# Sixty-four experts spread over 28 steps instead of 32, and eight output tiles normalised in a new order

## The chip, the cores and the metric

The kernel runs on one core of one Trainium2 chip. The metric is the device time of one execution in microseconds (us). A core has five engines with a program each: TensorE (PE, matmuls), VectorE (DVE), ScalarE (ACT), GpSimd (POOL) and SyncE (SP, which here only issues DMAs). They meet at semaphores: an instruction waits until a counter has reached a value, and raises another when it is done. Sixteen DMA engines move data for all of them.

## What is computed

A layer of a network on `x`, 4 sequences of 1024 tokens with 512 channels, so 4096 rows in all. First comes an attention-like part (a linear recurrence over time), with a norm and a residual; its result is called `x1`, and its layernorm `h`. The change touches only the second part, the feed-forward:

```
idx, wts = router(h)                       # 64 experts, 6 chosen for each token, weights wts
shared = relu2(h @ shared_up.T) @ shared_down.T          # 512 -> 1024 -> 512, every token
routed = for each expert e: its tokens (at most 128) through relu2(xd @ w1[e].T) @ w2[e].T,
         times wts, added into the row of each token     # 512 -> 256 -> 512
out = x1 + layernorm(shared + routed)
```

`relu2` is the square of relu. The sum over a token's experts and the shared part is formed in an array `ysh` in HBM and in SBUF, as told below.

## The kernel before

**Tiles and steps.** The 4096 rows are 8 row tiles of 512, each 4 sub-tiles of 128. The shared part runs over the tiles `k = 0..7`, and in each over 8 slices `j = 0..7` of the hidden 1024. One pass over `j` is a step here: TensorE does `up(k, j)` (12 matmuls, since each product is split into three of high and low parts), ScalarE takes relu and square (L980, L985), VectorE the square and the low part (`split`, L1607 and L1610), and two steps later TensorE does `down(k, j-2)` (12 matmuls) into `y_bank`. The last two `down` of a tile follow in its last step.

**Experts.** From tile 3 on (`ROUTED`), the experts are woven into the steps. `experts_until(step)` shares the 64 evenly over steps `FIRST_STEP` to `LAST_STEP`, 2 to 33, counted from tile 3 slice 0; so every step has exactly two, and the last are in tile 7, slice 1. One expert is: POOL gathers 128 token rows of `h` by an indirect DMA (L1170); TensorE transposes them (L661), multiplies by w1 (L672, 16 instructions in the profile) and by w2 (L683, 4); ScalarE copies, takes relu, and scales by the gate (L1008, L1014, L1022); VectorE squares and writes the lists of indices (L1633, L1624, L1626, L1617); then POOL adds the 128 result rows into `ysh` with a second indirect DMA (L1196).

**What orders the adds.** Two experts can have the same token, so each add waits on `added` until the one before has landed: on POOL the program is gather, add, gather, add, and the adds are strictly one behind the other. There are four result buffers (`EB`) and four sets of weights (`WB`). VectorE's L1624 for expert e waits for the add of expert e-4, ScalarE's L1022 likewise. The gather of expert e+5 stands just ahead of the add of expert e in POOL's program. SP loads the w1 half (512 KB) of expert e+5 when expert e+1 is through its first matmuls, and the w2 half of e+4 when e is done.

**The end.** When all 64 adds have landed (`added` = 16*64), the sum of a tile k can be made whole. The shared results of tiles 0 to 2 are already in `ysh`; those of tiles 3 to 6 lie in SBUF (`v_sb`, `hb`, `sr`, `xin`), that of tile 7 in PSUM. Before the change, tiles 0 to 2 are just loaded; 3 and 4 come by DMAs of POOL that add while they land (`add_sums`, L1207); 7, 5 and 6 are summed by TensorE with an identity matrix (`o_sum`, L750 and L751). Then per tile, in the order of `O_ORDER`: VectorE takes mean and variance (`o_moments`, L1705 to L1711), POOL the inverse deviation (L1216, L1218), ScalarE normalises (`o_norm`, L1083), POOL and VectorE add `x1`, two sub-tiles each (L1226, L1719), and SP stores. VectorE's first three `o_moments` stand in steps j = 5, 6, 7 of tile 7, each behind that step's `split`, and `o_add(n)` stands behind `o_moments(n+1)`. The last `down(7, 7)` waits for the `split` of step 7.

Of the kernel before, what the change touches and what calls it, by code (L numbers as in the profile page):

```python
# [35 lines left out]
FIRST_STEP, LAST_STEP = 2, SJ * (NT - 1 - ROUTED) + 1  # L36
TURN_STEP = {1: 0, 2: 3, 3: 6, 4: 9, 5: 12, 6: 14, 7: 18}

O_ORDER = [0, 1, 2, 3, 4, 7, 5, 6]
O_ADDED, O_SUMMED = (3, 4), (7, 5, 6)  # L40
# [6 lines left out]
def sandwich(nc, t):  # L47

    ctx = ExitStack()
    with ctx:  # L50
# [170 lines left out]
        def by_row_tile(w):  # L221
            return w.rearrange("p (s c) -> p s c", s=ST)

        o_y = [hT, xres[:, :, :], xnd[:, :, :], v_sb[:, :, :], hb[:, :, :]] + [by_row_tile(weights[:, n, :]) for n in (5, 6, 4)]
        o_from = o_y[:5] + [banks[0], y_bank, y_bank]
        o_x = [by_row_tile(wkv[:, n * ST * C:(n + 1) * ST * C]) for n in range(WB - 1)] + [by_row_tile(state_flat[:, 0:ST * C])] + \
              [by_row_tile(weights[:, n, :]) for n in (7, 0, 1)] + [rw[:, :, :]]
# [7 lines left out]
        out_by_tile = t["out"].rearrange("(t s p) c -> t p s c", s=ST, p=P)  # L235

# [65 lines left out]
        def _(sp):  # L302
# [121 lines left out]
            def load_x1(k):  # L424
                sp.dma_start(o_x[k], x1_by_tile[k]).then_inc(S[f"x1_loaded{k}"], 16)

            def load_sums(k):
                sp.dma_start(o_y[k], ysh_by_tile[k]).then_inc(S[f"ysh_loaded{k}"], 16)
# [36 lines left out]
            load_x1(7)  # L465
            store_out(1)
            sp.wait_ge(S["down_done"], SJ * NT)
            load_x1(5)
            store_out(2)
            load_x1(6)  # L470
            for n in range(3, NT):
                store_out(n)
            sp.wait_ge(S["out_stored"], 16 * NT)
# [3 lines left out]
        def _(pe):  # L477
# [262 lines left out]
            def o_sum(n, k):  # L740

                pe.wait_ge(S[f"ysh_loaded{k}"], 16)
                if k == 5:
                    pe.wait_ge(S["relu_ready"], SJ * NT)
                    pe.wait_ge(S["e_gated"], E)
                if k == 6:
                    pe.wait_ge(S["o_normed"], ST * (O_ORDER.index(7) + 1))
# [8 lines left out]
            for n, k in enumerate(O_SUMMED):  # L756
                o_sum(n, k)
# [3 lines left out]
        def _(act):  # L761
# [326 lines left out]
            for n in range(2, NT):  # L1088
                o_norm(n)
# [672 lines left out]
```

## Time and profile before

| what | us |
|---|---|
| median of the runs | 1297.98 |
| the runs shown | 1286.64, 1297.98, 1530.0 |
| the profiled execution | 1293.94 |
| its span, first to last instruction | 1292.3 |
| TensorE busy | 1174.3 (91%) |
| VectorE busy | 770.2 (60%) |
| adds of experts (L1196), first issue to last | 774.75 to 1221.79 |
| stores and norms at the end, after the last add landed | about 65 |

Times in the trace are from the start of the span. The span is what the rows add up to; the profiled execution's own time is 1.64 us more.

### The profile page before, as it was taken

The numbers are of one execution on the slowest core, as the hardware profiler recorded it, in microseconds if no ns is written. First come the engines' busy times: TensorE is split into PE (matmuls) and PEld (weight loads), VectorE is DVE, ScalarE is ACT, GpSimd is POOL, SyncE is SP. The second block draws the span as 40 slices with busy tenths as digits, with TensorE's granted clock in tenths as the row PEclk, the third lists the DMA queues.
The fourth block names the chain that finished last, engine by engine and source line by source line (L and its number), as shares of the span: only waits on it lengthen the run. The fifth ranks groups of instructions, "written<-read, shape, count | busy, mean of one in ns | idle before, by whom it ended". The sixth has DMA issues, their size and how long they took to land.

```text
span 1292.3 us, 15333 instructions
## 1 busy us (share of the span) xinstructions
PE 1174.3 (91%) x4952; PEld 765.3 (59%) x4952; DVE 770.2 (60%) x1965; ACT 595.8 (46%) x993; POOL 283.4 (22%) x268
## 2 busy tenths in 40 slices
PE   5997999999889995869999899999998999999974
PEld 2443444443334442458888777777776777777751
DVE  4598988988798998759898941222221222222274
ACT  2455657574757557753333133343342334334243
POOL 2010202020202001200000023333342433433255
PEclk9998999999999998879999999999999999999987
DMA  8401022322222222596424149879988898997698
GB/s 299 179 1 33 11 75 66 97 46 98 32 93 37 83 48 98 138 289 213 159 86 155 39 154 242 243 218 268 240 205 256 228 244 235 246 244 174 161 309 341
DMA packets 79517, 206.16 MB, mean 160 GB/s; under 512 B 10192, under 2 KB 10320, under 8 KB 76624
## 3 DMA queue, kind: packets, MB, share of 16 engines
q1 hardware_dynamic: 59408, 156.98, 35.8%
q0 software_dynamic: 20032, 48.24, 19.4%
q8 instruction: 37, 0.61, 0.2%
q14 instruction: 40, 0.33, 0.1%
HBM read 145.93 MB, written 59.28 MB: 159 GB/s over the span
## 4 chain that ended last, share of the span: by engine, by line
PE 37%; DMA 11%; DVE 6%; issue 2%; ACT 1%; POOL 1%; SPq 1%; POOLq 0%; DVEq 0%; ACTq 0%
PE bank L672 7%; PE bank L683 7%; DMA ysh<-k_sb,mixf 5%; PE bank L647 3%; PE bank L649 3%; PE bank L648 3%; DMA xres<-h,mixf 3%; PE bank L629 3%; PE bank L631 3%; PE bank L630 3%; PE bank L661 2%; DMA xnd<-ysh 2%; PE bank L491 1%; DMA xin<-h 1%; DVE stats L1705 1%
## 5 line engine op out<-in xcount | busy, mean ns | idle before, releaser
L534 PE MATMUL bank<-mix_ring,weights 128*128 128x512 f32 x768 | 344.2, 606 | 13.7 <-ACT xres L835 6.7
L534 PEld LDWEIGHTS bank<-mix_ring,weights 128*128 128x128 f32 x768 | 147.5, 194 | 199.4 <-issue 192.9
L1196 POOL DMA_INDIRECT ysh<-k_sb,mixf x64 | 102.0, 1594 | 225.3 <-DVE mixf L1617 135.2
L1607 DVE TENSOR_TENSOR k_sb<-k_sb 128x512 f32<-128x512 f32 x64 | 44.1, 688 | 152.9 <-ACT k_sb L980 142.7
L1633 DVE TENSOR_TENSOR run_max<-run_max 128x256 f32<-128x256 f32 x64 | 27.3, 426 | 175.6 <-ACT run_max L1014 175.5
L541 PE MATMUL bank<-weights,rw 128*128 128x512 f32 x256 | 117.5, 614 | 12.1 <-ACT sr L794 9.0
L647 PE MATMUL bank<-ffn_w,s_split 128*128 128x512 f32 x256 | 115.1, 450 | 5.4 <-DVE s_split L1610 5.4
L629 PE MATMUL bank<-h_high,ffn_w 128*128 128x512 f32 x256 | 114.1, 446 | 4.3 <-ACT k_sb L980 2.7
L980 ACT ACTIVATE k_sb<-bank 128x512 f32<-128x512 f32 x64 | 38.2, 597 | 170.8 <-PE bank L631 170.8
L649 PE MATMUL bank<-ffn_w,s_split 128*128 128x512 f32 x256 | 101.8, 398 | 0.0
L648 PE MATMUL bank<-ffn_w,s_split 128*128 128x512 f32 x256 | 101.7, 397 | 0.0
L631 PE MATMUL bank<-h_high,ffn_w 128*128 128x512 f32 x256 | 100.8, 394 | 0.0
L630 PE MATMUL bank<-h_low,ffn_w 128*128 128x512 f32 x256 | 100.4, 392 | 0.0
L1170 POOL DMA_INDIRECT xres<-h,mixf x48 | 48.7, 1014 | 228.3 <-DVE mixf L1617 213.8
L672 PE MATMUL bank<-xnT,wkv 128*128 128x128 f32 x768 | 96.2, 280 | 0.1
L541 PEld LDWEIGHTS bank<-weights,rw 128*128 128x128 f32 x256 | 50.1, 198 | 77.1 <-issue 65.4
L1107 POOL TENSOR_SCALAR rstd<-mv 128x4 f32<-128x4 f32 x16 | 9.9, 620 | 379.8 <-DVE mv L1259 371.7
L672 PEld LDWEIGHTS bank<-xnT,wkv 128*128 128x128 f32 x768 | 92.3, 197 | 0.3 <-issue 0.3
L683 PE MATMUL bank<-wkv,run_max 128*128 128x512 f32 x192 | 90.3, 593 | 0.0
L1022 ACT ACTIVATE k_sb<-bank,mixf 128x512 f32<-128x512 f32 x64 | 44.1, 689 | 86.3 <-PE bank L683 78.3
L1288 DVE SCALAR_TENSOR_TENSOR mix_ring<-xnd,vecs,xnT 128x512 f32<-128x512 f32 x96 | 70.1, 745 | 3.9 <-PE bank L534 1.9
L1008 ACT ACTIVATE xnT<-bank 128x512 f32<-128x512 f32 x64 | 37.7, 588 | 66.9 <-PE bank L661 66.8
(217 smaller groups left out, 2025.5 us busy)
## 6 DMA issues: line engine op xcount, KB each, us to landing
wkv<-in_w SPq DMA_DIRECT2D x96, 512.0 KB
state<-in_w SPq DMA_DIRECT2D x32, 512.0 KB
xin<-in_x SPq DMA_DIRECT2D x8, 1024.0 KB, 5.3
xin<-h SPq DMA_DIRECT2D x8, 1024.0 KB, 6.4
xres<-in_x POOLq DMA_DIRECT2D x7, 1024.0 KB, 9.4
h<-hb SPq DMA_DIRECT2D x7, 1024.0 KB, 4.3
x<-xres SPq DMA_DIRECT2D x7, 1024.0 KB, 7.0
ht<-xnT SPq DMA_DIRECT2D x7, 1024.0 KB, 8.5
```

Of the source, the lines that this page charges most:

```text
L534: mm = pe.matmul(bank[:, d, :], W(j)[:, ck, d * P:(d + 1) * P], mix_slot(4 * j + ck), start=(ck == 0), stop=(ck == CK - 1))
L541: mm = pe.matmul(bank[:, s, :], rw[:, ck, s * P:(s + 1) * P], W(3)[:, ck, :], start=(ck == 0), stop=(ck == CK - 1))
L629: pe.matmul(up_bank, hi, hT_hi[:, ck, :], start=(ck == 0), stop=False)
L630: pe.matmul(up_bank, hi, hT_lo[:, ck, :], start=False, stop=False)
L631: mm = pe.matmul(up_bank, lo, hT_hi[:, ck, :], start=False, stop=(ck == CK - 1))
L647: pe.matmul(y_bank[:, s, :], hi, w_hi, start=(j == 0), stop=False)
L648: pe.matmul(y_bank[:, s, :], hi, w_lo, start=False, stop=False)
L649: mm = pe.matmul(y_bank[:, s, :], lo, w_hi, start=False, stop=(j == SJ - 1 and k < NT - 1))
L672: mm = pe.matmul(e_up_bank[:, i * CAP:(i + 1) * CAP], w1_sb[e % WB][:, ck, i * P:(i + 1) * P], xdT[q][:, ck, :], start=(ck == 0), stop=(ck ...
L683: mm = pe.matmul(route_bank, e_act[b][:, i, :], w2_sb[e % WB][:, i, :], start=(i == 0), stop=(i == IK - 1))
L1196: pool.indirect_dma_start(t["ysh"], bass.IndirectOffsetOnAxis(ap=scatter_token[:, q:q + 1], axis=0), e_out[q], None, compute_op=ALU.add).t ...
L1288: dve.scalar_tensor_tensor(out=mix_slot(n), in0=xnd[:, ck, :], scalar=vecs[:, MK + j, ck:ck + 1], in1=xnT[:, ck, 0:TT], op0=ALU.mult, op1= ...
```

## The change

`LAST_STEP` falls from 33 to 29, so the 64 experts lie in 28 steps, two in most and three in eight of them; the last three are in tile 6, slice 5. The end goes through the tiles in the order 0, 3, 4, 1, 5, 2, 6, 7. Tiles 3 and 4 are loaded plainly into the free buffers of tiles 1 and 2 and added to the shared result by VectorE (`O_JOINED`, a new counter `o_joined`); tiles 1 and 2 are loaded into those buffers once they are free again. Tiles 5 and 6 come by POOL's adding DMAs (`O_ADDED`), issued behind the first `o_scale`. Only tile 7 is summed by TensorE, straight onto its PSUM bank. `x1` passes through four slots. VectorE's first six `o_moments` stand in steps j = 2 to 7 of tile 7, and ScalarE's `o_norm` from j = 3.

```diff
-FIRST_STEP, LAST_STEP = 2, SJ * (NT - 1 - ROUTED) + 1
+FIRST_STEP, LAST_STEP = 2, SJ * (NT - 2 - ROUTED) + 5
-O_ORDER = [0, 1, 2, 3, 4, 7, 5, 6]
-O_ADDED, O_SUMMED = (3, 4), (7, 5, 6)
+O_ORDER = [0, 3, 4, 1, 5, 2, 6, 7]
+O_JOINED, O_ADDED = (3, 4), (5, 6)
...
+        o_y = [hT, xres[:, :, :], xnd[:, :, :]] + [m[:, :, :] for m in youts[ROUTED:]] + [by_row_tile(weights[:, 4, :])]
+        o_from = o_y[:NT - 1] + [y_bank]
+        x1_slots = [by_row_tile(wkv[:, n * ST * C:(n + 1) * ST * C]) for n in range(WB - 1)] + [by_row_tile(state_flat[:, 0:ST * C])]
+        sums_of = dict(enumerate(o_y))
+        sums_of.update({3: o_y[1], 4: o_y[2]})
...
             sp.wait_ge(S["added"], 16 * E)
-            for k in range(ROUTED):
-                load_sums(k)
-            sp.wait_ge(S["up_done"], SJ * NT)
-            load_sums(7)
-            load_x1(4)
-            load_sums(5)
-            store_out(0)
-            load_sums(6)
...
+            load_sums(0)
+            load_sums(3)
+            load_sums(4)
+            sp.wait_ge(S["o_joined"], ST)
+            load_sums(1)
+            sp.wait_ge(S["o_joined"], ST * 2)
+            load_sums(2)
+            for n in range(NT):
                 store_out(n)
+                if n + WB < NT:
+                    load_x1(n + WB)
+                if n == 2:
+                    sp.wait_ge(S["up_done"], SJ * NT)
+                    load_sums(7)
...
-            for n, k in enumerate(O_SUMMED):
-                o_sum(n, k)
+            pe.wait_ge(S[f"ysh_loaded{NT - 1}"], 16)
+            for s in range(ST):
+                mm = pe.matmul(y_bank[:, s, :], ident[:, :], sums_of[NT - 1][:, s, :], start=False, stop=True)
+            mm.then_inc(S["o_summed"], 1)
...
-                    if k == NT - 1 and j >= SJ - 2:
-                        o_norm(j - (SJ - 2))
+                    if k == NT - 1 and j >= 3:
+                        o_norm(j - 3)
...
             for n in range(NT):
                 o_scale(n)
+                if n == 0:
+                    for k in O_ADDED:
+                        add_sums(k)
...
-                    if k == NT - 1 and j >= SJ - 3:
-                        o_moments(j - (SJ - 3))
-                    if k == NT - 1 and j >= SJ - 2:
-                        o_add(j - (SJ - 2))
+                    if k == NT - 1 and j >= 2:
+                        o_moments(j - 2)
+                    if k == NT - 1 and j >= 3:
+                        o_add(j - 3)
...
+                if k in O_JOINED:
+                    dve.wait_ge(S["yout_ready"], ST * (k + 1))
+                    for s in range(ST):
+                        dve.tensor_tensor(o_y[k][:, s, :], o_y[k][:, s, :], sums_of[k][:, s, :], ALU.add).then_inc(S["o_joined"], 1)
+                    dve.wait_ge(S["o_joined"], ST * (O_JOINED.index(k) + 1))
```

The first place is ScalarE's program in a step of tile 5: one step before the change. `k_sb<-bank0` and `s_split` are the shared part; each row that waits on `added` is the gate of one expert, after which POOL can add its rows into `ysh`.

```order
L980 ACTIVATE k_sb_61<-bank0 128x512 [waits square_ready,up_done]
L985 ACTIVATE s_split_52<-k_sb_61 128x512 [waits down_done,relu_ready]
L1008 ACTIVATE xnT_59<-bank0 128x512 [waits e_up,xd_turned]
L1014 ACTIVATE run_max_65<-bank0 128x256 [waits e_square,e_up]
L1022 ACTIVATE k_sb_61<-bank0,mixf_60 128x512 [waits added,scatter_index,e_down]
L1008 ACTIVATE xnT_59<-bank0 128x512 [waits e_up,xd_turned]
L1014 ACTIVATE run_max_65<-bank0 128x256 [waits e_square,e_up]
L1022 ACTIVATE k_sb_61<-bank0,mixf_60 128x512 [waits added,scatter_index,e_down]
```

And one of the eight steps with three experts, after the change:

```order
L971 ACTIVATE k_sb_61<-bank0 128x512 [waits square_ready,up_done]
L976 ACTIVATE s_split_52<-k_sb_61 128x512 [waits down_done,relu_ready]
L999 ACTIVATE xnT_59<-bank0 128x512 [waits e_up,xd_turned]
L1005 ACTIVATE run_max_65<-bank0 128x256 [waits e_square,e_up]
L1013 ACTIVATE k_sb_61<-bank0,mixf_60 128x512 [waits added,scatter_index,e_down]
L999 ACTIVATE xnT_59<-bank0 128x512 [waits e_up,xd_turned]
L1005 ACTIVATE run_max_65<-bank0 128x256 [waits e_square,e_up]
L1013 ACTIVATE k_sb_61<-bank0,mixf_60 128x512 [waits added,scatter_index,e_down]
L999 ACTIVATE xnT_59<-bank0 128x512 [waits e_up,xd_turned]
L1005 ACTIVATE run_max_65<-bank0 128x256 [waits e_square,e_up]
L1013 ACTIVATE k_sb_61<-bank0,mixf_60 128x512 [waits added,scatter_index,e_down]
```

A third expert stands in the same step, and each of its three gates still waits for the adds of earlier experts.

The second place is VectorE's program at the end, where the second tile of `O_ORDER` is taken: before the change in step j = 6 of tile 7 (`xres` is tile 1, `xnT` tile 0).

```order
L1607 TENSOR_TENSOR k_sb_61<-k_sb_61 128x512 [waits relu_ready]
L1610 TENSOR_TENSOR s_split_52<-k_sb_61,s_split_52 128x512 [waits s_hi_ready,square_ready]
L1705 BN_STATS stats_71<-xres_57 128x6 [waits ln4_moments,ysh_loaded1]
L1705 BN_STATS stats_71<-xres_57 128x6 x3
L1708 BN_AGGR mv_72<-stats_71 128x2 [waits ln4_stats]
L1708 BN_AGGR mv_72<-stats_71 128x2 x3
L1710 TENSOR_SCALAR rstd_73<-mv_72 128x4 [waits ln4_moments]
L1711 TENSOR_SCALAR offset_76<-mv_72 128x4
L1719 TENSOR_TENSOR xnT_59<-xnT_59,wkv_67 128x512 [waits o_normed,x1_loaded0]
L1719 TENSOR_TENSOR xnT_59<-xnT_59,wkv_67 128x512 [waits o_normed]
```

After the change it stands in step j = 3, and is tile 3 (`v_sb`), whose routed part has landed in `xres`:

```order
L1599 TENSOR_TENSOR k_sb_61<-k_sb_61 128x512 [waits relu_ready]
L1602 TENSOR_TENSOR s_split_52<-k_sb_61,s_split_52 128x512 [waits s_hi_ready,square_ready]
L1694 TENSOR_TENSOR v_sb_62<-v_sb_62,xres_57 128x512 [waits yout_ready,ysh_loaded3]
L1694 TENSOR_TENSOR v_sb_62<-v_sb_62,xres_57 128x512 x3
L1702 BN_STATS stats_71<-v_sb_62 128x6 [waits ln4_moments,o_joined]
L1702 BN_STATS stats_71<-v_sb_62 128x6 x3
L1705 BN_AGGR mv_72<-stats_71 128x2 [waits ln4_stats]
L1705 BN_AGGR mv_72<-stats_71 128x2 x3
L1707 TENSOR_SCALAR rstd_73<-mv_72 128x4 [waits ln4_moments]
L1708 TENSOR_SCALAR offset_76<-mv_72 128x4
L1716 TENSOR_TENSOR xnT_59<-xnT_59,wkv_67 128x512 [waits o_normed,x1_loaded0]
L1716 TENSOR_TENSOR xnT_59<-xnT_59,wkv_67 128x512 [waits o_normed]
```

Four adds of 128x512 (L1694) have come between the `split` and the moments, and three more steps of the shared part now stand behind this place.

## Rows read from the trace of the kernel before

**Rows 1.** The page: TensorE's busy time; DMA busy tenths in 40 slices.

```profile
PE 1174.3 (91%) x4952; PEld 765.3 (59%) x4952; DVE 770.2 (60%) x1965; ACT 595.8 (46%) x993; POOL 283.4 (22%) x268
DMA  8401022322222222596424149879988898997698
```

**Rows 2.** Chain of waits, 1015:1035: start us, us, what. TensorE's pace.

```profile
1018.29 1.79 PE bank L672 x16
1024.98 1.79 PE bank L672 x16
```

**Rows 3.** Chain of waits, 1110:1250: three of the last five adds.

```profile
1192.65 8.02 DMA ysh<-k_sb,mixf
...
1201.53 7.70 DMA ysh<-k_sb,mixf
...
1221.79 4.82 DMA ysh<-k_sb,mixf
```

**Rows 4.** Timeline of POOL, adds of experts: start, us, line, [idle before <-releaser].

```profile
774.75 1.65 POOL L1196 DMA_INDIRECT ysh<-k_sb,mixf  x1 [0.30 <-issue]
...
859.38 1.59 POOL L1196 DMA_INDIRECT ysh<-k_sb,mixf  x1 [0.39 <-issue]
868.27 1.59 POOL L1196 DMA_INDIRECT ysh<-k_sb,mixf  x1 [5.33 <-DVE mixf L1617]
879.81 1.59 POOL L1196 DMA_INDIRECT ysh<-k_sb,mixf  x1 [8.66 <-DVE mixf L1617]
```

**Rows 5.** Line L1196 in the stretches 879:968 and 1120:1188: count, first and last start.

```profile
L1196 POOL DMA_INDIRECT ysh<-k_sb,mixf x14: 1587/1589/1605, 879.8 to 966.8; - x14
...
L1196 POOL DMA_INDIRECT ysh<-k_sb,mixf x11: 1587/1589/1590, 1120.5 to 1186.8; - x11
```

**Rows 6.** Timeline of ACT: gates of the first expert, the 61st, 62nd, and last.

```profile
772.10 0.69 ACT L1022 ACTIVATE k_sb<-bank,mixf 128x512 f32<-128x512 f32 x1 [1.34 <-PE bank L683]
...
1192.46 0.69 ACT L1022 ACTIVATE k_sb<-bank,mixf 128x512 f32<-128x512 f32 x1 [1.33 <-PE bank L683]
1196.40 0.69 ACT L1022 ACTIVATE k_sb<-bank,mixf 128x512 f32<-128x512 f32 x1 [1.34 <-PE bank L683]
...
1205.46 0.69 ACT L1022 ACTIVATE k_sb<-bank,mixf 128x512 f32<-128x512 f32 x1 [2.14 <-PE bank L683]
```

**Rows 7.** Timeline of ACT: relu in steps without experts.

```profile
1213.64 0.60 ACT L980 ACTIVATE k_sb<-bank 128x512 f32<-128x512 f32 x1 [4.18 <-PE bank L631]
...
1219.08 0.60 ACT L980 ACTIVATE k_sb<-bank 128x512 f32<-128x512 f32 x1 [4.18 <-PE bank L631]
```

**Rows 8.** Waits in 760:1227: who waited for whom, us in total, times, longest.

```profile
DVE mixf L1624 <- DMA ysh<-k_sb,mixf: 37.6, 32, 6.6
...
PE bank L661 <- DMA xres<-h,mixf: 10.3, 6, 4.4
```

**Rows 9.** Stretches: PE, PEld, DVE, ACT, POOL busy, PEclk, DMA share, GB/s.

```profile
1120.00:1186.00 66.00, 66.00 (x350) 51.20 (x349) 14.88 (x48) 22.26 (x41) 26.18 (x20) 1.00 0.89 235
...
1227.00:1252.00 25.00, 19.08 (x74) 14.94 (x73) 15.69 (x39) 8.20 (x12) 9.90 (x9) 0.86 1.01 272
```

**Rows 10.** Timeline of DVE from 1226: the end.

```profile
1232.26 2.47 DVE L1705 BATCH_NORM_STATS2 stats<-xnT 128x6 f32<-128x512 f32 x4 [5.69 <-DMA xnT<-ysh]
...
1235.34 0.68 DVE L1607 TENSOR_TENSOR k_sb<-k_sb 128x512 f32<-128x512 f32 x1
...
1244.31 1.79 DVE L1610 TENSOR_TENSOR s_split<-k_sb,s_split 128x512 fp32r<-128x512 f32 x1
...
1255.88 2.46 DVE L1705 BATCH_NORM_STATS2 stats<-hb 128x6 f32<-128x512 f32 x4
...
1260.19 2.47 DVE L1705 BATCH_NORM_STATS2 stats<-bank 128x6 f32<-128x512 f32 x4
...
1276.88 2.49 DVE L1705 BATCH_NORM_STATS2 stats<-bank 128x6 f32<-128x512 f32 x4 [8.03 <-PE bank L751]
```

**Rows 11.** Timeline of POOL: an add of x1 in the same stretch.

```profile
1244.29 2.94 POOL L1226 TENSOR_TENSOR xnT<-xnT,wkv 128x512 f32<-128x512 f32 x2
```

More of the change, by code:

```diff
@@ L222, in by_row_tile @@
             return w.rearrange("p (s c) -> p s c", s=ST)
[L224 to L227, printed above, removed]
+        o_y = [hT, xres[:, :, :], xnd[:, :, :]] + [m[:, :, :] for m in youts[ROUTED:]] + [by_row_tile(weights[:, 4, :])]
[3 more added lines that the diff above has]
+        sums_of.update({3: o_y[1], 4: o_y[2]})
         x_by_tile = t["x"].rearrange("(t s p) c -> t p s c", s=ST, p=P)
@@ L235, in sandwich, with o_x @@
         out_by_tile = t["out"].rearrange("(t s p) c -> t p s c", s=ST, p=P)
+        def o_x(n):
+            return x1_slots[n % WB]
         def o_slot(n):
@@ L422, in _, with load_x1 @@
             store_shared(ROUTED - 1)
-            def load_x1(k):
-                sp.dma_start(o_x[k], x1_by_tile[k]).then_inc(S[f"x1_loaded{k}"], 16)
+            def load_x1(n):
+                sp.dma_start(o_x(n), x1_by_tile[O_ORDER[n]]).then_inc(S[f"x1_loaded{n}"], 16)
             def load_sums(k):
-                sp.dma_start(o_y[k], ysh_by_tile[k]).then_inc(S[f"ysh_loaded{k}"], 16)
+                sp.dma_start(sums_of[k], ysh_by_tile[k]).then_inc(S[f"ysh_loaded{k}"], 16)
             def store_out(n):
@@ L738, in tile @@
                     table_add(NT - 1)
[L740 to L747, printed above, removed]
-                for s in range(ST):
-                    if k != 7:
-                        pe.matmul(o_from[k][:, s, :], ident[:, :], youts[k][:, s, :], start=True, stop=False)
-                    mm = pe.matmul(o_from[k][:, s, :], ident[:, :], o_y[k][:, s, :], start=False, stop=True)
-                mm.then_inc(S["o_summed"], 1)
             for k in range(NT):
                 tile(k)
-            for n, k in enumerate(O_SUMMED):
-                o_sum(n, k)
+            pe.wait_ge(S[f"ysh_loaded{NT - 1}"], 16)
+            for s in range(ST):
+                mm = pe.matmul(y_bank[:, s, :], ident[:, :], sums_of[NT - 1][:, s, :], start=False, stop=True)
+            mm.then_inc(S["o_summed"], 1)
         @block.scalar
@@ L1087, in _ @@
                 tile(k)
-            for n in range(2, NT):
+            for n in range(SJ - 3, NT):
                 o_norm(n)
@@ L1207, in add_sums @@
                 pool.dma_start(o_y[k], ysh_by_tile[k], accum_op=ALU.add).then_inc(S[f"ysh_loaded{k}"], 16)
-            for k in O_ADDED:
-                add_sums(k)
             def o_scale(n):
@@ L1222, in o_add @@
                 k = O_ORDER[n]
-                pool.wait_ge(S[f"x1_loaded{k}"], 16)
+                pool.wait_ge(S[f"x1_loaded{n}"], 16)
                 for s in range(ST // 2):
                     pool.wait_ge(S["o_normed"], ST * n + s + 1)
-                    pool.tensor_tensor(o_y[k][:, s, :], o_y[k][:, s, :], o_x[k][:, s, :], ALU.add).then_inc(S["o_ready"], 1)
+                    pool.tensor_tensor(o_y[k][:, s, :], o_y[k][:, s, :], o_x(n)[:, s, :], ALU.add).then_inc(S["o_ready"], 1)
             for n in range(NT):
                 o_scale(n)
+                if n == 0:
+                    for k in O_ADDED:
+                        add_sums(k)
                 if n >= 1:
@@ L1715, in o_add @@
                 k = O_ORDER[n]
-                dve.wait_ge(S[f"x1_loaded{k}"], 16)
+                dve.wait_ge(S[f"x1_loaded{n}"], 16)
                 for s in range(ST // 2, ST):
                     dve.wait_ge(S["o_normed"], ST * n + s + 1)
-                    dve.tensor_tensor(o_y[k][:, s, :], o_y[k][:, s, :], o_x[k][:, s, :], ALU.add).then_inc(S["o_added"], 1)
+                    dve.tensor_tensor(o_y[k][:, s, :], o_y[k][:, s, :], o_x(n)[:, s, :], ALU.add).then_inc(S["o_added"], 1)
             for k in range(NT):
                 tile(k)
-            for n in range(3, NT):
+            for n in range(SJ - 2, NT):
                 o_moments(n)
```

11 lines of the change are left out of this document (2 added, 9 removed).

## The prediction

> **What bounds the kernel now.** I read the page first: TensorE is busy for 91% of the span, and the DMA engines are at 8 or 9 tenths in most slices from the 25th on [rows 1]. A kernel like that invites the reading "TensorE is the bound, everything else hides behind it". The chain of waits says the same for the middle: one expert follows the other at 1024.98 - 1018.29 = 6.69 us, by TensorE's own instructions [rows 2]. But at the end the chain is another one: the adds of experts into `ysh`, each released by the landing of the one before (1192.65 + 8.02 = 1200.67, the next starts at 1201.53: 0.86 us between), down to the last landing at 1221.79 + 4.82 = 1226.6 [rows 3]. So I laid the adds [rows 4, 5] beside the gates that feed them [rows 6]. The first add starts 2.65 us after its gate; the last one 1221.79 - 1205.46 = 16.3 us after its own. The adds fall behind in one burst (859.38, 868.27, 879.81: services of 8.9 and 11.5 us) and do not come back: from 879.8 to 966.8 there are 13 services of 6.69 us, from 1120.5 to 1186.8 ten of 6.63 [rows 5]. In such a stretch the adds are back to back, at the same pace as TensorE, so both are at their limit together. That the queue is full shows in VectorE too: L1624, which waits for the add four experts back, was held 32 times for 37.6 us, and TensorE waited 6 times for a gather that stands behind an add on POOL, 10.3 us [rows 8]. That is the view on which this forecast rests: **TensorE has the work, but the adds are a second chain of nearly the same length.**
>
> **Costs on TensorE.** The expert alone costs 1196.40 - 1192.46 = 3.94 us [rows 6]. A step without experts is 1219.08 - 1213.64 = 5.44 us, so a block of `up` or `down` is 2.72 us [rows 7]. Check: 2.72 + 3.94 = 6.66, against 6.69. No TensorE work is removed by the new spread; four steps' worth (8 blocks, 21.8 us) move behind the experts. With no wait, the last gate would come after 63 x 3.94 + 55 x 2.72 = 397.8 us, at 1169.9, where it now comes after 433.4 us [rows 6]. That would be 6.31 us an expert.
>
> **Costs on the chain of adds.** Per add: 4.82 us to land when nothing else moves [rows 3], plus the 0.86 us, is 5.7 us, the lower bound. The steady value beside two loads of weights, a gather and a DMA share of 0.89 [rows 9] is 6.65 us. Which one? The change keeps 1 MB of weights and one gather for each add, so if TensorE is held back by the adds the DMA engines stay just as full, and I take 6.65. Now all 63 services take 1221.79 - 774.75 = 447.0 us [rows 3, 4]; 63 x 6.65 = 419.0, so 28 us are extra. Of these about 5 us are idle time before 859.38 (84.6 us for 12 services is 5 over 79.8), as TensorE at a tile's end does `down` blocks and feeds nothing; the other 23 us are bursts behind such a pause, at four tile boundaries (5.7 us each; the first is (8.9 + 11.5) - 2 x 6.65 = 7.1). After the change the experts cross three boundaries, 17 us; the idle time goes, since the adds are a little behind by then; and in the first eleven services I allow 2 us, as some of that pace is TensorE's. Chain: 419.0 + 17 - 2 = 434 us, so the **last add starts at 1209 instead of 1221.8 and lands at 1214.**
>
> **When the end can begin.** The first sums were in SBUF 1232.26 - 1226.6 = 5.7 us after the last landing [rows 10]; that gives 1219.6. But VectorE meets the first `o_moments` behind the `split` of step 2 of tile 7. From the last gate to there TensorE has nine blocks, 24.5 us, two waits for the relu between `up` blocks with nothing between them, and relu and split, 4 us (an estimate from 0.60 us for the relu and twice 0.68 for the split [rows 7, 10], with a pause of 1 us for each wait): 28.5. The last gate runs 16 to 17 us ahead of the last add, since the gather of an expert stands five adds ahead and I take the lag seen [rows 3, 6]: 1192.5 + 28.5 = 1221. TensorE, not the load, sets this: **1221**, against 1232.3.
>
> **The end itself.** VectorE now needs 60.0 us from there to the end of the span. A tile costs 1260.19 - 1255.88 = 4.31 us: 3.08 for the moments (1232.26 to 1235.34), the rest two adds [rows 10]. After the change: first moments 3.1; steps 3 and 4 with a split (1.4), four joins of the same shape as the split (4 x 0.69 = 2.8), moments and adds, 8.5 each; steps 5, 6, 7 without joins 5.75 each; tile 6, 4.3; that is 41.7 us to the moments of tile 7. Against that stands what goes: the 8.03 us that VectorE waited for TensorE's `o_sum` [rows 10], as one matmul group stays of three. From the moments of the last tile to the end it is 1292.3 - 1276.9 = 15.4, unchanged. Sum 57.1 us. For the loads that share the DMA engines I add 1 us (their share is 1.01 already in 1227 to 1252 [rows 9]). The joins stand beside POOL's adds of x1. In the trace one such meeting made a VectorE operation of 128x512, 0.68 us else, 1.79 us long [rows 10], while POOL's pair ran from 1244.29 for 2.94 us [rows 11]: 1.1 us for a meeting, and with two joined tiles I put 2.2 us. End stage: 60.3 us.
> The Trainium skill ("SBUF — State Buffer", Who interferes with whom) holds that a VectorE instruction with two SBUF inputs and a reading GpSimd instruction take one port pair for the whole instruction, and the loser blocks. By that rule each joined tile could wait for two whole adds of POOL, and the sum would be 1 to 3 us longer; the row agrees in kind.
> `up` and `down` of tile 7 hide behind VectorE here (5.44 us a step against 5.75 or more); if VectorE were quicker they would be next, at 1192.5 + 22 x 2.72 = 1252 for the last `down`, plus some 18 us: 1270 at the earliest. The adding loads of tiles 5 and 6 have some 25 and 35 us until they are read. The x1 loads and the stores are the same number as before.
>
> **Sum.** 1221 + 60.3 = 1281.3 of span, plus 1.64, is **1283 us**, against 1293.94 for the profiled execution: 0.8% less. The median shown is 1297.98, with 1286.64 beside it, so two undisturbed runs of the same program differ by as much as I forecast. About 2% is what a measurement can tell from no change.
>
> **Rivals.**
> 1. *TensorE's pace.* The adds get quicker when they are asked for sooner: the lock at 6.69 us would be a matter of when the weights are loaded, and 5.7 us is possible. For it: in the first stretch adds kept up with the gates. Against it: 40 services in a row with a queue behind them did not shorten. Last gate at 1170, + 28.5 + 60 = 1258.5, **1260 us**. Intermediate values, a service of 6.4, give -16 us: 1267. Chance of 1268 or less: 0.24.
> 2. *Bursts in the new steps (slower).* Two experts of a three-expert step stand with nothing between them, so their weights, 2 MB, are asked for within 4 us. If each of the eight steps slows the adds as a tile boundary does, 5.7 us each, it is 46 us: 1329. It takes over from 1.4 us a step (then nothing is left of the gain) and is slower by 2% from 4.6 us. Against it: with the adds behind, TensorE cannot run the three at its own pace. A half of it, 3.4 us a step, gives **1310**. Chance of slower by 2%: 0.07.
> The Trainium skill ("DMA: Bandwidth & Descriptors", Latency and other measured facts) gives an access to HBM 0.2 us on average and 2 us at high load; 1.8 us on each add in the eight steps would be 14 us and take the whole gain. The landing of 4.82 us alone against 8.02 us beside loads [rows 3] agrees in kind.
> 3. *The gain isn't there.* The adds set the end, and their chain comes out as long as now, 447 us: the end stage starts at 1232 again and is no shorter, 1292 to **1296 us**. For it: the boundaries' bursts may only move. Chance 0.25, within my class of no change.
>
> **Chances and range.** Forecast around 1283 (1272 to 1290): 0.44; faster by more 0.24; no gain 0.25; slower 0.07. From -2% to +2%: 0.69. The range leaves out the lower half of rival 1 and rival 2: 1262 to 1300, for a service between 6.3 and 6.9 us.
>
> **What would show it.** Adds back to back from the third or fourth step on, services of 6.6 to 6.7 us outside the boundaries, L1616 held for more than 37.6 us in all, TensorE waiting for gathers for more than 10.3; last add near 1209; the first moments near 1221, ended by TensorE and not by a load; no wait of 8 us for the sums of tile 7. Wrong, if the last gate comes before 1180, or the adds leave their queue empty, or a load of sums holds VectorE in the end stage, or the end stage takes over 64 us.

## The result: about 4 us slower, where 11 us of gain were forecast

| | before | after |
|---|---|---|
| median (20 runs each, in turn on one chip) | 1288.43 | 1293.82 |
| lowest | 1283.62 | 1289.21 |
| ratio, 95% interval | | 1.0033 [1.0018, 1.0048] |
| profiled execution, its span | 1293.94, 1292.3 | 1292.89, 1291.2 |

The comparison leaves disturbed runs such as the 1530.0 out. The median lies within 2% of the time before and in the range of 1262 to 1300, but on the other side of "no change" than the 1283 that was forecast: 1.0033 of 1288.43 is +4.2 us, with an interval of +2.3 to +6.2. (The ratio is the comparison's own estimate and not the quotient of the two medians, which differ by 5.4 us.) The two profiled executions are 1 us apart, the other way round. The first lesson stands in that: the profiled execution of before lay 5.5 us above the median of its own 20 runs.

**The chain of adds, after.** In the profile after, L1187 is the add, L1013 the gate, L1609 and L1616 VectorE's copies of indices. First POOL's timeline: start, duration, line, and in brackets the idle time before and what ended it.

```profile
777.58 1.65 POOL L1187 DMA_INDIRECT ysh<-k_sb,mixf  x1 [0.30 <-issue]
...
1196.25 1.55 POOL L1187 DMA_INDIRECT ysh<-k_sb,mixf  x1 [4.91 <-DVE mixf L1618]
1202.73 1.55 POOL L1187 DMA_INDIRECT ysh<-k_sb,mixf  x1 [4.93 <-DMA ysh<-k_sb,mixf]
1208.39 1.62 POOL L1187 DMA_INDIRECT ysh<-k_sb,mixf  x1 [4.11 <-DMA ysh<-k_sb,mixf]
1214.17 1.55 POOL L1187 DMA_INDIRECT ysh<-k_sb,mixf  x1 [4.16 <-DMA ysh<-k_sb,mixf]
```

They answer to [rows 3, 4]. A service is the time from the start of one add to the start of the next: 63 services took 1214.17 - 777.58 = 436.6 us, against 447.0 before and 434 forecast. The first add starts 2.8 us later than before. That is scatter: over all the profiles below, the first add starts between 773.3 and 779.6. The gates, from ScalarE's timeline, answer to [rows 6]:

```profile
774.92 0.69 ACT L1013 ACTIVATE k_sb<-bank,mixf 128x512 f32<-128x512 f32 x1 [1.34 <-PE bank L686]
...
1197.75 0.69 ACT L1013 ACTIVATE k_sb<-bank,mixf 128x512 f32<-128x512 f32 x1 [2.14 <-PE bank L686]
```

The last gate runs 16.4 us ahead of its add, as before (16.3). Who waits for the adds, in 760 to 1227 (us in total, times, longest), against [rows 8]:

```profile
DVE mixf L1616 <- DMA ysh<-k_sb,mixf: 43.9, 34, 4.8
...
PE bank L664 <- DMA xres<-h,mixf: 14.5, 10, 3.2
```

Both waits grew, from 37.6 and 10.3 us. In the second profiles (run 11) the first of them is 28.1 us before and 50.0 after, so its growth repeats: TensorE asks for more experts in the time, and the queue of adds holds it more.

**The end, after.** VectorE's timeline, which answers to [rows 10]. L1599 and L1602 are `split`, L1694 the joins of tiles 3 and 4, L1702 the moments, L1716 the adds of `x1`.

```profile
1226.18 2.47 DVE L1702 BATCH_NORM_STATS2 stats<-xnT 128x6 f32<-128x512 f32 x4
...
1230.27 0.69 DVE L1599 TENSOR_TENSOR k_sb<-k_sb 128x512 f32<-128x512 f32 x1 [0.94 <-ACT k_sb L971]
1231.01 0.69 DVE L1602 TENSOR_TENSOR s_split<-k_sb,s_split 128x512 fp32r<-128x512 f32 x1
1231.62 2.49 DVE L1694 TENSOR_TENSOR v_sb<-v_sb,xres 128x512 f32<-128x512 f32 x4
...
1239.13 1.82 DVE L1602 TENSOR_TENSOR s_split<-k_sb,s_split 128x512 fp32r<-128x512 f32 x1
1240.88 3.59 DVE L1694 TENSOR_TENSOR hb<-hb,xnd 128x512 f32<-128x512 f32 x4
1244.50 2.48 DVE L1702 BATCH_NORM_STATS2 stats<-hb 128x6 f32<-128x512 f32 x4
...
1256.19 1.81 DVE L1602 TENSOR_TENSOR s_split<-k_sb,s_split 128x512 fp32r<-128x512 f32 x1
...
1275.87 2.49 DVE L1702 BATCH_NORM_STATS2 stats<-bank 128x6 f32<-128x512 f32 x4 [2.60 <-PE bank L747]
```

And POOL beside it, which answers to [rows 11]:

```profile
1239.12 3.00 POOL L1215 TENSOR_TENSOR xnT<-xnT,wkv 128x512 f32<-128x512 f32 x2
...
1256.17 2.99 POOL L1215 TENSOR_TENSOR hb<-hb,wkv 128x512 f32<-128x512 f32 x2
...
1273.78 2.49 POOL L1215 TENSOR_TENSOR xnd<-xnd,wkv 128x512 f32<-128x512 f32 x2
```

Read the second halves of the splits. At 1231.01 POOL is idle and L1602 takes 0.69 us. At 1239.13 and 1256.19 POOL starts its pair of adds 0.01 or 0.02 us ahead, L1602 takes 1.8, and POOL's pair 3.0 instead of 2.49. There are four such splits (1249.50 and 1262.90 are the others), and the join at 1240.88 is 1.10 us longer than the one at 1231.62. That is 4 x 1.12 + 1.10 = 5.6 us. Runs 4 and 5 test this by cutting POOL's adds. The wait of 8.03 us for TensorE's sums is a wait of 2.60 now. The chain of waits says why it is still there:

```profile
1260.15 10.23 DMA weights<-ysh
1270.39 0.04 issue
1270.43 5.41 PE bank L747 x8
```

SP asks for tile 7's sums only behind the store of tile 4 (1259.18), the load takes 10.2 us beside full DMA engines, and TensorE's eight instructions take 5.4 us. The stretches show both (columns as in [rows 9]):

```profile
1240.00:1280.00 40.00, 27.59 (x95) 19.22 (x93) 36.85 (x83) 20.12 (x30) 24.33 (x23) 0.85 1.04 362
...
1270.00:1280.00 10.00, 5.40 (x8) 2.03 (x8) 7.27 (x23) 5.42 (x8) 6.68 (x7) 0.73 1.02 393
```

The DMA share is 1.04, and the granted clock falls to 0.73 in the stretch in which TensorE has only the eight. In run 3, where they come without an idle time ahead of them and at a granted clock of 1.00, the same eight take 3.60 us. The end stage, from the first moments to the end, is 1291.2 - 1226.2 = 65.0 us, against 60.0 before and 60.3 forecast.

### The profile page after: what moved, and what is told of

It reads as the page before. It is cut to its first block, busy times and chain, and to the rows that moved or that the text cites. A ratio compares the mean times of both kernels' runs of the same rounds, so it can differ in the third digit from the quotient of the medians.

```text
span 1291.2 us, 15276 instructions
## 1 busy us (share of the span) xinstructions
PE 1160.8 (90%) x4920; PEld 757.5 (59%) x4920; DVE 779.0 (60%) x1973; ACT 596.7 (46%) x993; POOL 285.5 (22%) x268
## 4 chain that ended last, share of the span: by engine, by line
PE 24%; DMA 21%; DVE 6%; issue 3%; POOL 2%; ACT 1%; SPq 1%; POOLq 0%; DVEq 0%; ACTq 0%
DMA ysh<-k_sb,mixf 16%; PE bank L675 3%; PE bank L686 3%; PE bank L650 2%; PE bank L652 2%; PE bank L651 2%; PE bank L632 2%; PE bank L634 2%; PE bank L633 2%; DMA xres<-h,mixf 2%; PE bank L494 1%; DMA xnd<-h,mixf 1%; DMA xin<-h 1%; PE bank L664 1%; DMA weights<-ysh 1%
## 5 line engine op out<-in xcount | busy, mean ns | idle before, releaser
L1187 POOL DMA_INDIRECT ysh<-k_sb,mixf x64 | 102.2, 1596 | 233.8 <-DVE mixf L1609 117.5
L1599 DVE TENSOR_TENSOR k_sb<-k_sb 128x512 f32<-128x512 f32 x64 | 44.0, 688 | 131.8 <-ACT k_sb L971 121.8
L650 PE MATMUL bank<-ffn_w,s_split 128*128 128x512 f32 x256 | 112.9, 441 | 1.3 <-DVE s_split L1602 1.2
L652 PE MATMUL bank<-ffn_w,s_split 128*128 128x512 f32 x256 | 101.4, 396 | 0.0
L651 PE MATMUL bank<-ffn_w,s_split 128*128 128x512 f32 x256 | 101.1, 395 | 0.0
L1098 POOL TENSOR_SCALAR rstd<-mv 128x4 f32<-128x4 f32 x16 | 10.5, 657 | 382.3 <-DVE mv L1251 374.1
L1013 ACT ACTIVATE k_sb<-bank,mixf 128x512 f32<-128x512 f32 x64 | 44.1, 689 | 86.3 <-PE bank L686 72.9
```

Of the source, the lines that this page charges most:

```text
L650: pe.matmul(y_bank[:, s, :], hi, w_hi, start=(j == 0), stop=False)
L651: pe.matmul(y_bank[:, s, :], hi, w_lo, start=False, stop=False)
L652: mm = pe.matmul(y_bank[:, s, :], lo, w_hi, start=False, stop=(j == SJ - 1 and k < NT - 1))
L1187: pool.indirect_dma_start(t["ysh"], bass.IndirectOffsetOnAxis(ap=scatter_token[:, q:q + 1], axis=0), e_out[q], None, compute_op=ALU.add).t ...
```

## Experiments

The times are medians; ratios are to the kernel before, run in turn with each. In the profiles of all: the 63 services (first add's start to the last's), and the end stage as above.

**1. The spread alone.**

```diff
-FIRST_STEP, LAST_STEP = 2, SJ * (NT - 1 - ROUTED) + 1
+FIRST_STEP, LAST_STEP = 2, SJ * (NT - 2 - ROUTED) + 5
```

> The kernel before with LAST_STEP = 29 alone: 28 steps, the old end. Theory (the adds are a chain of their own, and TensorE's shared part now stands between them and the end): the last add starts some 8 us earlier than in the kernel before, but the first moments stand in step 5 of tile 7, behind 15 blocks of 2.72 us from the last gate (40.8 us and some 5 us of relu waits and split), so they begin near 1243 instead of 1232. From there it is 60 us less the 3.8 us of waits for loads: about 1297 to 1300, 4 to 8 us over the kernel before. Rival (TensorE's total work sets the time, order does not matter): the same as before within 2 us.

1305.88 us, 1.0095 [1.0065, 1.0126]. The services took 445.3 us, but look at VectorE behind the last add, which started at 1224.1:

```profile
1241.27 0.69 DVE L1607 TENSOR_TENSOR k_sb<-k_sb 128x512 f32<-128x512 f32 x1 [4.01 <-ACT k_sb L980]
...
1246.71 0.69 DVE L1607 TENSOR_TENSOR k_sb<-k_sb 128x512 f32<-128x512 f32 x1 [4.01 <-ACT k_sb L980]
1247.44 0.69 DVE L1610 TENSOR_TENSOR s_split<-k_sb,s_split 128x512 fp32r<-128x512 f32 x1
1248.05 2.47 DVE L1705 BATCH_NORM_STATS2 stats<-xnT 128x6 f32<-128x512 f32 x4
```

The first moments stand in slice 5 here and come 24.0 us behind the last add (10.5 before), at TensorE's pace of 5.44 us a step. They were expected near 1243 and came at 1248, and the whole lies above the expected 1297 to 1300: the theory holds, at a higher price. The blocks that the spread moves behind the experts have to be paid unless the end begins in an earlier slice. So the new place of the moments is a condition of the spread, not an extra.

**2. The new end alone**, with the old 32 steps.

```diff
-FIRST_STEP, LAST_STEP = 2, SJ * (NT - 2 - ROUTED) + 5
+FIRST_STEP, LAST_STEP = 2, SJ * (NT - 1 - ROUTED) + 1
```

> The changed kernel with LAST_STEP = 33: the new end with the old 32 steps. Theory: the last add lands where it did before (near 1226), the first moments wait in step 2 of tile 7 for the load behind it, to 1232, and VectorE holds TensorE back meanwhile; then the 65 us of the changed kernel's end stage follow: 1297 of span, 8 to 10 us over the kernel before. Rival (the new end is no longer than the old, and the loss lies in the spread): the same as before within 2 us.

1295.41 us, 1.0035 [1.0008, 1.0061]: the whole loss, and no less than with the spread (1.0033). The end stage was 65.1 us, as in after. The loss is smaller than the 8 to 10 us expected, and the first moments came at 1226.5 and not at 1232, since the chain of this execution took 441.2 us. So at this end the spread brought nothing that 12 to 20 runs can tell, and the new end costs what was lost.

**3. Tile 7's sums loaded early.**

```diff
+        last_sums = k_sb[:, :, 2:4, :]
...
+            for a in range(2):
+                sp.dma_start(last_sums[:, a], ysh_by_tile[NT - 1][:, 2 * a:2 * a + 2, :]).then_inc(S[f"ysh_loaded{NT - 1}"], 16)
```

> The changed kernel, with the routed sums of tile 7 loaded right behind those of tiles 0, 3 and 4 into the four result buffers of the experts, which are free by then, in two DMAs of 512 KB; no wait for up_done on SP. Theory (VectorE's 2.60 us wait at the end is for this load, which took 10.2 us from a late issue): 2 to 3 us less than the changed kernel. Rival (TensorE's last matmuls at the low clock set that wait): less than 1 us. Second rival (1 MB more at the start of the end stage delays the sums of tiles 3 and 4): 0 to 2 us more.

1291.36 us, 1.0003 [0.9981, 1.0024]. End stage 62.4 us, 2.6 less than after, and no wait ahead of tile 7's moments:

```profile
1258.15 1.84 DVE L1602 TENSOR_TENSOR s_split<-k_sb,s_split 128x512 fp32r<-128x512 f32 x1
...
1268.47 2.48 DVE L1702 BATCH_NORM_STATS2 stats<-bank 128x6 f32<-128x512 f32 x4
```

The 2.6 us were a real wait, and the late load was its cause. The rival (TensorE's last matmuls at the low clock) is no cause of its own: the eight instructions take 3.60 us here and 5.40 in after, so the load that came late brought their slowness with it.

**4. POOL's adds cut to 8 of 512 columns.**

```diff
-                    pool.tensor_tensor(o_y[k][:, s, :], o_y[k][:, s, :], o_x(n)[:, s, :], ALU.add).then_inc(S["o_ready"], 1)
+                    pool.tensor_tensor(o_y[k][:, s, 0:8], o_y[k][:, s, 0:8], o_x(n)[:, s, 0:8], ALU.add).then_inc(S["o_ready"], 1)
```

> The changed kernel, with POOL adding x1 to 8 of 512 columns only in its two sub-tiles of each tile, so most of that half of the residual is left out. Theory (POOL's adds and VectorE's two-input operations exclude each other; four splits and one group of joins are 1.1 us longer each for it): VectorE's end stage is 5 to 6 us shorter up to the last tile's moments, and the last tile's own adds save 1 to 2 us more: 6 to 8 us less than the changed kernel. Rival (the end stage is held by DMA traffic or by TensorE): 0 to 2 us less.

1295.14 us, 1.0018 [0.9992, 1.0043]: against after nothing can be told, where 6 to 8 us less were expected. The trace tells where it went. VectorE reached tile 6 in 38.4 us (42.7 after), and then stood:

```profile
1258.68 0.72 DVE L1602 TENSOR_TENSOR s_split<-k_sb,s_split 128x512 fp32r<-128x512 f32 x1
...
1274.45 2.49 DVE L1702 BATCH_NORM_STATS2 stats<-bank 128x6 f32<-128x512 f32 x4 [6.51 <-PE bank L747]
```

The splits are back at 0.72 us, and what they gave went into the wait for tile 7 (6.51 instead of 2.60): tile 7's moments come 49.3 us behind the first, 49.7 in after. The end stage is 62.4 us all the same, 2.6 less, but 2.2 of that lie behind tile 7's moments, where POOL's own last adds are nearly gone. Two costs lie one behind the other. The late load hides what POOL's contention costs; contention does not hide the late load, as run 3 shows.

**5. Both at once** (the edits of 3 and 4).

> ysh7_early with POOL's adds of x1 cut to 8 of 512 columns (most of half the residual is left out). In small_pool_adds VectorE reached the moments of tile 6 4 us sooner, and then waited for TensorE and the late load; here that load is early. Theory (the two engines exclude each other): first to last moments 43 us, against 47.1 in ysh7_early, and 2 us less at the end, so about 6 us less than ysh7_early. Rival (TensorE's pace in tile 7 sets the stretch): 45 us or more.

1287.35 us, 0.9965 [0.9944, 0.9986], though its profile has the longest chain of all the 28-step profiles but one (446.9 us). From the first moments to tile 7's it took 40.5 us, where 3 took 47.1: 5.6 us of contention, and a pause of 0.9 us for a relu that an end beginning late does not have. The end stage is 56.9 us. It falls by 5.5 and not by 6.6, since the last store takes 7.4 us, where it takes 4.2 in after: with VectorE this quick, the DMA engines (share 1.05 in 1256 to 1286) are likely the next to hold the end. POOL's pair is out of the way in 0.8 us:

```profile
1258.05 0.32 POOL L1207 TENSOR_TENSOR offset<-offset,rstd 128x4 f32<-128x4 f32 x1
1258.32 0.81 POOL L1215 TENSOR_TENSOR hb<-hb,wkv 128x8 f32<-128x8 f32 x2
```

**6. Two adds in flight.** Odd experts add into a second array with a counter of its own, which is left out of the result.

```diff
-                else:
-                    pool.wait_ge(S["added"], 16 * e)
+                if e >= 2:
+                    pool.wait_ge(*added(e - 2))
...
-                pool.indirect_dma_start(t["ysh"], ...
+                pool.indirect_dma_start(t["ysh2"] if e % 2 else t["ysh"], ...
```

> The changed kernel, in which the adds of odd experts go into a second array with a counter of their own, so that two adds may be in flight; what lands there is left out of the result, and the second array is blanked at the start by nine stores. Theory (adds back to back bound the expert stretch; TensorE would be quicker): the last gate comes 20 to 28 us earlier than in the changed kernel (near 1172), the last add within 8 us of it, and the end stage of 65 us starts when TensorE reaches it, near 1201: a span of 1266, 25 us less. Rival (the DMA engines are full, so the adds only share what there is): each add takes longer to land as two are in flight, the last add moves by less than 8 us, the time by less than 8.

1267.55 us, 0.9821 [0.9784, 0.9857]. ScalarE's timeline has the last gate, POOL's the last add:

```profile
1170.21 0.69 ACT L1021 ACTIVATE k_sb<-bank,mixf 128x512 f32<-128x512 f32 x1 [2.14 <-PE bank L694]
```

```profile
1168.88 1.55 POOL L1195 DMA_INDIRECT ysh<-k_sb,mixf  x1 [4.71 <-ACT k_sb L1021]
1171.72 1.55 POOL L1195 DMA_INDIRECT ysh<-k_sb,mixf  x1 [1.29 <-ACT k_sb L1021]
```

The prediction had put TensorE's own pace at a last gate of 1169.9; it is 1170.2. POOL's adds wait for the landing of an earlier add once, for 5.1 us (in after 11 times, for 47.0 us). An add takes no less time than before, 6.0 us in the median, so it is the rule of one at a time, at the price that an add has beside the weights, that keeps the expert stretch above 397 us. Some 26 us of the whole are in it.

**7. Two adds in flight and 32 steps** (the edits of 6 and 2).

> The changed kernel with two adds in flight (odd experts add into a second array, which is left out of the result) and the experts over 32 steps, not 28. It tells what the spread is worth where the adds do not bind. Theory (TensorE's pace is then the bound, and the number of blocks between the first and the last gate sets it): 63 x 3.94 + 63 x 2.72 = 419.6 us from the first gate to the last, 23 us more than in the 28-step variant (396.3 us); behind the last gate one block less of waiting: VectorE meets the first moments some 10 to 13 us after the last gate at the earliest, set by the load of the sums; the two shifts nearly cancel and the whole is within 5 us of the 28-step variant (1262 to 1273 us). Rival (the gain of the 28-step variant came from the spread and the second array together, the adds still bind at 32 steps): first to last gate over 430 us, whole over 1280.

1274.48 us, 0.9865 [0.9841, 0.9888]. The stretch came as expected, the whole 1.5 us above the 1262 to 1273 given. First to last gate 1194.42 - 774.1 = 420.3 us against 419.6 worked out:

```profile
1194.42 0.69 ACT L1021 ACTIVATE k_sb<-bank,mixf 128x512 f32<-128x512 f32 x1 [2.14 <-PE bank L694]
```

So where the adds do not bind, the spread does what it says: from the first gate to the last it takes 22.2 us less (398.1). Of that 0.9865 - 0.9821 = 0.0044, some 6 us, reaches the end, as the first moments come 28.4 us behind the last gate with 28 steps and 13.9 with 32. The intervals of the two overlap a little; the four runs of each do not (1263.2 to 1268.8, 1272.8 to 1276.2).

**8. The weights loaded in their first eighth.** One add in flight, 28 steps; experts from the fifth on compute with stale weights.

```diff
-                sp.dma_start(dst[e % WB].rearrange("p k i -> p (k i)"), t[name][e]).then_inc(S[f"{name}_loaded{e % WB}"], 16)
+                cols = 1024 if e < WB else 128
+                sp.dma_start(dst[e % WB].rearrange("p k i -> p (k i)")[:, 0:cols], t[name][e][:, 0:cols]).then_inc(S[f"{name}_loaded{e % WB}"], 16)
```

> The changed kernel, with the weights of experts 4 to 63 loaded only in their first eighth (64 KB of 512 KB for each of the two arrays); what these experts compute is left out of consideration, they use stale weights. Everything else, the one add in flight and the 28 steps too, is as in the changed kernel. Theory (an add takes 4.8 us alone and 5.5 to 10 us only because the weights of an expert move beside it): the adds land in 4.8 to 5.2 us, a service is 5.7 to 6.1 us, they keep up with TensorE, lag at the end under 4 us, first to last gate 396 to 400 us as with two adds in flight, the whole 1262 to 1272 us. Rival 1 (the slowness is the adds' own: their writes into rows that the add before has just touched, or POOL's share): services stay at 6.3 to 6.9 us on average, first to last gate above 420 us, the whole 1285 to 1298. Rival 2 (half and half): first to last gate 400 to 420 us.

1268.96 us, 0.9842 [0.9808, 0.9876]. An add lands in 4.9 us in the median (5.7 or 5.8 in the seven profiles of one add in flight and full weights that give a median), and first to last gate is 1175.1 - 777.0 = 398.1 us. Where adds queue, most follow at 5.6 to 5.9 us:

```profile
1121.96 1.59 POOL L1188 DMA_INDIRECT ysh<-k_sb,mixf  x1 [4.89 <-DVE mixf L1610]
...
1127.57 1.59 POOL L1188 DMA_INDIRECT ysh<-k_sb,mixf  x1 [2.73 <-DMA ysh<-k_sb,mixf]
```

```profile
1120.00:1186.00 66.00, 65.13 (x331) 49.52 (x330) 12.85 (x45) 21.68 (x39) 22.85 (x16) 1.00 0.62 138
```

The DMA engines move 138 GB/s here, where after has 235 in the same stretch. The lag at the end was 9.3 us, not under 4: single adds still took up to 8.3 us, the last ones beside the loads of `x1`. So the adds are slow because the weights move beside them, and rival 1 of this run, a cost of their own, is out. Either the rule of run 6 or this traffic can go, and TensorE's pace sets the gates.

**9. x1 of five tiles added by DMAs** of POOL's queue, on top of 3. The three other tiles of `x1` are loaded plainly.

```diff
+BY_DMA = 5
...
+                if n < BY_DMA:
+                    pool.wait_ge(S["o_normed"], ST * (n + 1))
+                    pool.dma_start(o_y[k], x1_by_tile[k], accum_op=ALU.add).then_inc(S[f"x1_loaded{n}"], 16)
+                    return
```

> ysh7_early, and x1 of the first five tiles of the order added by DMAs of POOL's queue that add in SBUF behind the normalisation, so neither VectorE nor POOL adds them; three tiles of x1 are loaded plainly. Theory (the end stage is bound by VectorE, with POOL in its way): steps 5 to 7 fall from 6.7 us to TensorE's 5.44, first to last moments from 47.1 to about 40 us; 5 to 8 us less than ysh7_early, 3 to 6 less than the kernel before. Rival (the end is DMA traffic, at a share of 1.0 already): the adding loads hold back sums and stores, and the time is the same as ysh7_early or 5 us more.

1302.68 us, 1.0099 [1.0067, 1.0131], more even than its rival had given. VectorE reached tile 7 in 41.1 us instead of 47.1, and the stores came late. SP's issues, each store waiting for its tile's adding DMA:

```profile
1261.95 0.38 SPq L444 DMA_DIRECT2D out<-v_sb  x1
1269.98 0.37 SPq L444 DMA_DIRECT2D out<-hb  x1
1277.98 0.37 SPq L444 DMA_DIRECT2D out<-xres  x1
1286.01 0.37 SPq L444 DMA_DIRECT2D out<-sr  x1
```

The adding loads of 1 MB landed 8.0 us apart, 16 to 23 us after their issue: the bound moved from VectorE to them. The DMA share is 1.10 in 1256 to 1286, at 265 GB/s, so whether their queue or the DMA engines set the 8.0 us is not separated.

**10. The same for two tiles only**, stores in the order 2, 0, 3, 1, 4 to 7; meant to beat both kernels.

```diff
-BY_DMA = 5
+BY_DMA = 2
+STORE_ORDER = (2, 0, 3, 1, 4, 5, 6, 7)
```

> The variant with tile 7's sums loaded early, and x1 of the first two finished tiles added by adding DMAs instead of by VectorE and POOL; stores of finished tiles in the order 2, 0, 3, 1, 4 to 7. A version meant to beat both. Theory (VectorE's work and its meetings with POOL set the end stage, and only a long row of adding DMAs costs it back): the first moments to the eighth 47.1 - 2 x 1.4 - 2 x 1.1 = 42 us, from there to the end 16 to 19, end stage 59 to 61 instead of 62.4, the whole 1286 to 1290 us where the variant with early sums alone had 1291.4 in the median. Rival (the DMA engines, at a share of 1.0 in this stage, set its end, and adding DMAs take about 8 us each whatever their number): the stores end no earlier than now, end stage 62 to 66, the whole 1291 to 1296.

1292.45 us, 1.001 [0.9986, 1.0033]. A miss. VectorE was freed of two tiles' meetings, but was held for tile 1's sums instead. It reached tile 7 in 45.4 us (47.1 in run 3, 42 expected), the stores cost 1.7 us more behind that, and the end stage stayed at 62.4 us:

```profile
1250.93 2.47 DVE L1713 BATCH_NORM_STATS2 stats<-xres 128x6 f32<-128x512 f32 x4 [4.03 <-DMA xres<-ysh]
```

No version that computes the whole result beat the kernel before; 3 and 10 are level with it.

**11. Both kernels once more**, unchanged, one execution each.

> The kernel before once more, for a second trace. The profiled execution of it lay 5 us over the median of its runs. Theory (the expert stretch varies): the 63 services of the adds take 440 to 443 us here instead of 447.0, all else equal, and the span is 1286 to 1289. Rival: the extra 5 us lay before the expert stretch or in the end stage.

1292.21 us: services 445.9, where 440 to 443 were expected, and end stage 57.8, where the first profile has 60.0. The wait for TensorE's sums is 6.34 us here, 8.03 there.

> The changed kernel once more, unchanged, for the spread of one execution to the next. Theory (the adds' chain varies by itself by some 5 us, the end stage does not): 63 services between 436 and 446 us, the end stage from the first moments to the end 65 us within 1 us, since it is made of fixed steps; span 1286 to 1301. Rival (the 436.6 us of the first profile belong to the change): services 436 to 437.5 again, span 1290 to 1292.

1301.66 us: services 447.4, just above the 446 expected, end stage 65.9. In after the end stage repeats within 1 us and the chain does not (436.6 and 447.4). In before the chain repeats within 1.1 us and the end stage does not (60.0 and 57.8). The longest service of this profile is 1140.56 - 1129.70 = 10.86 us, that of the 51st expert, the first of tile 6:

```profile
1129.70 1.59 POOL L1187 DMA_INDIRECT ysh<-k_sb,mixf  x1 [6.44 <-DVE mixf L1609]
...
1140.56 1.64 POOL L1187 DMA_INDIRECT ysh<-k_sb,mixf  x1 [7.98 <-DVE mixf L1609]
```

## Why the prediction was wrong, step by step

**What bounds: right.** The adds are a second chain of nearly TensorE's length. Run 6 takes it away and the stretch falls to 397 us, TensorE's pace to within 1 us. Run 8 shows that the traffic of the weights beside them sets the price of an add.

**The chain's new length (434 us): right for one profile, too short for the kernel, and the first step that failed.** The steady service of 6.65 us was about right. But the chain's length varies by itself: with 32 steps it was 447.0, 445.9 and 441.2 us, with 28 steps and all weights loaded 436.6, 447.4, 445.3, 436.8, 437.3, 446.9, 439.3 and 442.3. Their means are 444.7 and 441.5: a gain of 3 us where 13 were forecast, and even that is within the scatter. Of the missing 10 us, 2.3 come from the start: 447.0 was the longest chain of three. The rest shows when the prediction's own sum, 6.65 us a service and what comes on top, is set against the adds' starts in these eleven profiles (the edits of runs 1 to 5, 9 and 10 that they belong to leave the order of the adds alone). A boundary is the last step of a tile and the first two of the next:

| us over 6.65 a service | forecast before | 32 steps, mean of 3 | forecast after | 28 steps, mean of 8 |
|---|---|---|---|---|
| first steps of tile 3 | 0 | -0.4 | -2 | +2.4 |
| boundary of tiles 3 and 4, with the idle time | 10.7 | 11.8 | 5.7 | 4.4 |
| tiles 4 and 5 | 5.7 | 6.0 | 5.7 | 4.6 |
| tiles 5 and 6 | 5.7 | 4.6 | 5.7 | 4.9 |
| tiles 6 and 7 | 5.7 | 1.2 | none | none |
| all other steps | 0 | 2.5 | 0 | 6.3 |

The idle time at the first boundary did go, as forecast. Three terms failed: the fourth boundary, which the spread takes out, cost 1.2 us and not 5.7; the first steps lost 2.4 us where 2 were to be gained; and 3.8 us more were lost in steps away from any boundary, which the prediction put at nothing. In the first steps it is one step with three experts (7 to 9) that costs 3.0 us; in run 8, with less traffic, the service of the 8th expert is 5.6 us, here 9.0 in the mean. So rival 2's mechanism is there, but how much of the 3.8 us is its work is open. Counted by the services of their own adds, the four later three-expert steps away from a boundary are at -0.3 to +0.3 us; counted by the time in which TensorE runs them, they cost the chain 0.7 to 2.0 us each. The longest services, those of the 14th, 33rd and 51st expert (9.2, 9.9 and 9.2 us in the mean of the eight), belong to the boundaries, and the last two stand in steps with two experts. Rival 3 (no gain on the chain) came nearest, with its 1296. The working that the prediction put under rival 2 for HBM accesses (14 us) charges one add in each of the eight steps; three in each, 24 in all, would have been 43 us.

**The first moments (1221): right in what sets them, 5 us off in time.** TensorE set them, not the load: 28.4 us behind the last gate in the profile (28.5 forecast), and 28.4 in run 6. They came at 1226.2, since the last gate was at 1197.8 and not 1192.5. Where the chain is long the load sets them again (second profile: 10.2 us behind the last add).

**The end stage (60.3 us): wrong, and the second step that failed.** It took 65.0, 65.9 and, in run 2, 65.1 us, over the 64 that the prediction had named as a sign of being wrong. VectorE's own work was right: 49.7 us to tile 7's moments, less 5.6 of contention and 2.6 of waiting, is 41.5 against 41.7 (with a pause of 0.9 us for a relu in it that was not in the sum). Two terms failed:
- Contention was put at 2.2 us, one meeting for each joined tile. In fact POOL's pair meets the `split` of each of four steps, and one join. The meeting was priced right (1.1 us) and counted wrong: the very row it was taken from, in [rows 10], is a `split` and not a join. The Trainium skill ("SBUF — State Buffer", Who interferes with whom) says that a VectorE instruction with two inputs in SBUF contends with a GpSimd instruction that reads SBUF. `split`'s subtraction has two such inputs, so by that rule each step was to be charged; the trace agrees, 0.69 us alone and 1.8 beside POOL's pair. The prediction applied the rule to the new instructions alone.
- The wait for TensorE's sums was held to be gone. It became 2.6 us (4.5 in the second profile), for a load that stands on SP behind a store that waits for the third finished tile (run 3).

The 1 us that the prediction added for loads sharing the DMA engines did not show beside these two: 3.4 + 2.6 - 1 is 5.0, about the 4.7 us that were missed.

Neither failed step turns the sign alone: the chain's missing 10 us by themselves leave a gain of 1, the end stage's 5 leave one of 6. Run 2 shows all the same that the loss comes with the new end, and with the old 32 steps too.

**The sum.** The forecast went from 1293.94, the profiled execution; the medians of before in the five comparisons were 1288.4 to 1293.0. By means of profiles instead: chain 441.5 - 444.7 = -3, end stage 65.5 - 58.9 = +6.6 (two profiles each) make +3.4, against a measured +4.2 [+2.3, +6.2]. With a chain that varies by 10 us, a fit this close is in part luck.

**What stays open.** Which of the transfers makes a single service take 8 to 11 us, why the same program has a chain of 437 us in one execution and 447 in the next, and where the 3.8 us away from the boundaries come from. That the spread is worth 3 us with one add in flight is not shown; that it is worth some 6 with two is likely.

## What to carry to other kernels

A chain of transfers that each wait for the one before is a bound of its own even when the engine beside it is 91% busy. Moving compute shortened it here by less than it varies; find what traffic each link shares and take away that, or the serial rule. When a change puts an engine's instructions where another engine works, charge contention to every instruction of both that now overlap, the old ones too. And before a gain under 1% is forecast from one profile, ask how much the stage varies between two profiles of the same program.

## What was not expected of the hardware

- An indirect adding DMA of 128 rows lands in 4.9 us in the median with little traffic beside it and in 5.7 or 5.8 at some 240 GB/s, but two in flight at once let the stretch run at TensorE's pace with nearly the same DMA share (0.90 and 258 GB/s in 780 to 1165, against 0.89 and 244 in after): the share said nothing about room for a second one.
- Adding loads of 1 MB on POOL's queue followed each other at 8.0 us in an end stage in which plain loads and stores of the same size kept pace with VectorE's 6.7 us a tile.
- A meeting of VectorE and POOL costs both: 0.69 to 1.8 us for the one instruction, 2.49 to 3.0 for POOL's pair.
